# Talking-heads attention and a gated transformer on one core: mixers scaled by GpSimd, 1+exp on ScalarE, a new order of the steps

## Chip, cores and metric

The kernel runs on 1 core of a Trainium2 chip. The metric is the device time of one execution in microseconds (us); less is better.

## What is computed

Sixteen batches of 512 tokens with 256 features go through two branches. One is an attention with 16 heads of size 16, in which a 16 x 16 matrix mixes the heads before the softmax and another after it. The other is a two-layer transformer with local attention (8 heads of size 64, window of 128) and a gated feed-forward part. The second branch's output x goes through a sigmoid and gates the first.

```python
# talking heads, for each batch
logits = einsum('bhid,bhjd->bhij', rope(q), rope(k)) * SCALE
logits = einsum('bhij,gh->bgij', logits, Wpre)
attn = softmax(logits, axis=-1)
attn = einsum('bhij,gh->bgij', attn, Wpost)
out = einsum('bhij,bhjd->bhid', attn, v)      # then @ Wout.T + bout
# gate, for each of 2 layers
x = x + local_attention(l2norm(q), l2norm(k), v) @ wo
h = layernorm(shift_token(x)) @ w1 + b1
a, g = split(h); x = x + (a * gelu(g)) @ w2 + b2
# at the end: attention output times silu(x), added to the input
```

## The kernel before

Each engine runs its own instruction stream, written out by hand with semaphores. The work of a batch is cut into some 330 named steps. `ORDER` is one list of all steps of a batch (lines 124 to 156); `FIRST_ORDER` and `LAST_ORDER` are the lists of the first and the last batch. Every engine walks through the same list and issues its own part of each step, so that the list sets the order in each of the five queues. Steps in `AHEAD` belong to the next batch, steps in `BEHIND` (bound, sigmoid, silu, gated, store) to the batch before. An engine's queue is in order: an instruction that waits holds all behind it.

**Talking heads.** A tile of scores has 8 query tokens x 16 mixed heads = 128 rows and 512 keys; there are 64 tiles (`scores.0` to `scores.63`). `expand` (GpSimd, L1487) makes the queries times the mixing weights for two tiles, in two products; `part` splits them into a rounded part (ScalarE, L979) and a rest (GpSimd, L1492), three chunks ahead at most. `scores` is six matmuls (L711 to 713), a maximum on VectorE (L1220), and Exp with the row sums on ScalarE (L992). For a pair of tiles, `mixers.m` takes the reciprocal of the row sums of tiles 2m and 2m+1 on VectorE (L1206), and then multiplies the post-softmax mixing matrix by them, also on VectorE (L1211): one product of 2 x 128 elements in each row, into `mixer_n`, which has two buffers. `mix.m` is 64 small matmuls of `probs` with `mixer_n` (L728); its two banks are copied out by ScalarE and VectorE (L553). `values` (L747) and `project` (L755) follow.

**Gate.** `qkv` is 18 matmuls into banks F0 to F2; VectorE multiplies by the rotation tables (L1243), ScalarE squares, VectorE sums (L1251) and clips (L1257), GpSimd takes the power -0.5 (`inv_norms`, L1503). `join` adds the rotated halves (VectorE, L1271) and scales k (GpSimd, L1510). `q_turn` and `k_turn` (L787) transpose. `local_scores` (L805) is followed by a masked minimum on VectorE (L1303), four Exps (ScalarE, L1042), and in `weigh` a reciprocal (VectorE, L1323) and a product over 128x1024 elements (GpSimd, L1518). `p_turn` transposes (L820, copied by L1314 and L1051), `local_values` (L836, copied into `o_locT` by L1332), `out_proj` (L848). `up` with gelu and `down` (L915) end the layer.

**Output gate.** `bound` clips x (VectorE, L1420) and takes exp(-x) (ScalarE, L1099); `sigmoid.t`, four times, adds 1 (L1425) and takes the reciprocal (L1427) on VectorE. `silu` and `gated` are products on GpSimd (L1535, L1540), `store` is a DMA from GpSimd's queue (L1545).

Of the kernel before, what the change touches and what calls it, by code (L numbers as in the profile page):

```python
# [134 lines left out]
part.11 scores.20 expand.12 local_values.0.5 p_turn.0.6 part.12 mix.9 out_proj.0.2 expand.13 local_values.0.6
p_turn.0.7 scores.21 local_values.0.7 mixers.10 scores.22 part.13 out_proj.0.3 mix.10 half_turn.0 scores.23
shift_turn.0 mixers.11 project.0 scores.24 scores.25 mix.11 expand.14 part.14 h_scale.0 mixers.12 scores.26 values.2
h_turn.0 expand.15 scores.27 part.15 scores.28 expand.16 mix.12 up.0.0 up.0.1 up.0.2 up.0.3 mixers.13 part.16 up.0.4
up.0.5 scores.29 mix.13 expand.17 mixers.14 down.0.0 down.0.1 down.0.2 down.0.3 mix.14 part.17 expand.18 x_turn.1
part.18 scores.30 scores.31 expand.19 qkv.1.0 join.1.0 scores.32 mixers.15 qkv.1.1 q_turn.1.0 k_turn.1.0 part.19  # L140
scores.33 join.1.1 scores.34 mix.15 mixers.16 qkv.1.2 k_turn.1.1 join.1.2 values.3 scores.35 expand.20 q_turn.1.1
mix.16 mixers.17 part.20 qkv.1.3 q_turn.1.2 k_turn.1.2 project.1 expand.21 join.1.3 scores.36 part.21 scores.37 mix.17
scores.38 q_turn.1.3 expand.22 part.22 mixers.18 k_turn.1.3 scores.39 mix.18 local_scores.1.0 mixers.19 scores.40
scores.41 mix.19 mixers.20 local_scores.1.1 weigh.1.0 expand.23 scores.42 part.23 values.4 local_scores.1.2 p_turn.1.0
scores.43 expand.24 weigh.1.1 weigh.1.2 scores.44 mix.20 local_scores.1.3 mixers.21 local_values.1.0 p_turn.1.1
scores.45 scores.46 mix.21 local_scores.1.4 local_values.1.1 weigh.1.3 mixers.22 part.24 p_turn.1.2 weigh.1.4
scores.47 local_scores.1.5 mix.22 expand.25 out_proj.1.0 scores.48 weigh.1.5 mixers.23 local_values.1.2 part.25
p_turn.1.3 mix.23 local_scores.1.6 local_values.1.3 scores.49 p_turn.1.4 expand.26 mixers.24 part.26 scores.50
out_proj.1.1 local_values.1.4 expand.27 values.5 local_scores.1.7 mix.24 weigh.1.6 weigh.1.7 p_turn.1.5 scores.51
# [9 lines left out]
expand.0 part.0 expand.1 part.1 expand.2 qkv.0.0 part.2 join.0.0 expand.3 scores.0 scores.1 qkv.0.1 q_turn.0.0  # L159
k_turn.0.0 join.0.1 scores.2 mixers.0 qkv.0.2 mix.0 scores.3 join.0.2 q_turn.0.1 mixers.1 part.3 k_turn.0.1 expand.4  # L160
qkv.0.3 k_turn.0.2 q_turn.0.2 scores.4 join.0.3 scores.5 mix.1 part.4 scores.6 mixers.2 q_turn.0.3 k_turn.0.3 scores.7
expand.5 mix.2 part.5 mixers.3 local_scores.0.0 expand.6 scores.8 scores.9 weigh.0.0 local_scores.0.1 mix.3 scores.10
p_turn.0.0 weigh.0.1 part.6 expand.7 local_scores.0.2 values.0 local_values.0.0 mixers.4 part.7 p_turn.0.1 weigh.0.2
scores.11 mix.4 expand.8 sigmoid.0 local_scores.0.3 local_values.0.1 weigh.0.3 mixers.5 scores.12 p_turn.0.2 scores.13
part.8 expand.9 mix.5 local_scores.0.4 mixers.6 out_proj.0.0 local_values.0.2 local_scores.0.5 p_turn.0.3 scores.14
scores.15 weigh.0.4 mix.6 part.9 weigh.0.5 local_scores.0.6 local_values.0.3 mixers.7 p_turn.0.4 scores.16 mix.7
expand.10 local_scores.0.7 local_values.0.4 out_proj.0.1 weigh.0.6 weigh.0.7 scores.17 p_turn.0.5 mixers.8 scores.18
p_turn.0.6 part.10 local_values.0.5 values.1 expand.11 local_values.0.6 store out_proj.0.2 scores.19 mix.8 p_turn.0.7
part.11 expand.12 scores.20 silu mixers.9 bound part.12 local_values.0.7 scores.21 expand.13 out_proj.0.3 mixers.10
mix.9 half_turn.0 scores.22 part.13 shift_turn.0 mix.10 scores.23 scores.24 expand.14 mixers.11 part.14 expand.15  # L170
project.0 h_scale.0 scores.25 scores.26 mix.11 mixers.12 gated h_turn.0 values.2 scores.27 scores.28 mix.12 part.15
mixers.13 up.0.0 sigmoid.1 up.0.1 up.0.2 expand.16 up.0.3 part.16 scores.29 mix.13 up.0.4 up.0.5 expand.17 part.17
mixers.14 scores.30 scores.31 expand.18 down.0.0 down.0.1 down.0.2 down.0.3 mixers.15 mix.14 x_turn.1 scores.32 mix.15
part.18 qkv.1.0 join.1.0 qkv.1.1 join.1.1 q_turn.1.0 values.3 k_turn.1.0 expand.19 scores.33 qkv.1.2 k_turn.1.1
# [117 lines left out]
def gate_network_kernel(nc, a, out):  # L292
# [9 lines left out]
    with ExitStack() as ctx:  # L302
# [629 lines left out]
        def _(act):  # L932
# [717 lines left out]
```

## Time and profile before

| | us |
|---|---|
| median of 3 runs | 5370.03 |
| lowest, highest | 5368.29, 5371.4 |
| the profiled execution | 5372.07 |
| its span, first to last instruction | 5370.0 |
| busy TensorE (PE) | 5119.1 |
| busy VectorE (DVE) | 3692.1 |
| busy ScalarE (ACT) | 2659.8 |
| busy GpSimd (POOL) | 2619.2 |

The profile is of one execution. PE is TensorE with its matmuls, PEld its weight loads. The matmuls' ends are modelled, and they overlap. The granted clock is 0.994 of full speed over the span. The batches are alike, about 331 us each in the middle of the run; batch 7 (counted from 0) has its first qkv step at 2376.8 us.

### The profile page before, as it was taken

To read this page: it belongs to the slowest core of one execution; us is meant where nothing else is said; L and a number is where in the kernel's file an instruction comes from. 1 tells how busy PE (TensorE), PEld (TensorE's weight loads), DVE (VectorE), ACT (ScalarE), POOL (GpSimd) and SP (SyncE) were. 2 spreads that over 40 slices of the span, in tenths; PEclk is the share of its full clock that TensorE was granted. 3 is DMA by queue.
4 is the path that set the end of the run, shared out by engine and by line. 5 is a ranking of instruction groups with operands and counts; after the bars stand their busy time and mean duration, and the time that the engine had idled before them with its cause. 6 is when DMAs were issued, how large, how long until landed. Compare 5 with 4: busy or idle time off the path is not lost. (4 is left out here: it accounts for less than half of the span.)

```text
span 5370.0 us, 176617 instructions
## 1 busy us (share of the span) xinstructions
PE 5119.1 (95%) x72856; PEld 4155.2 (77%) x72856; DVE 3692.1 (69%) x8889; ACT 2659.8 (50%) x6551; POOL 2619.2 (49%) x2308
## 2 busy tenths in 40 slices
PE   6999999999999999999999999999999999999998
PEld 5887777877778777787777777777777777777776
DVE  6667676667766667666676666766667676676765
ACT  4445554455544454544545445454455544555544
POOL 4445554445544445444464444544445444454543
PEclk9999999999999999999999999999999999999999
DMA  2211111121111111111110111101111011111110
GB/s 79 95 66 63 46 35 64 45 67 42 38 61 56 57 41 38 61 61 53 40 64 35 61 53 51 58 31 61 54 50 58 30 61 62 42 58 39 52 49 17
DMA packets 51388, 280.78 MB, mean 52 GB/s; under 512 B 5280, under 2 KB 22688, under 8 KB 33696
## 3 DMA queue, kind: packets, MB, share of 16 engines
q1 hardware_dynamic: 39840, 252.69, 12.8%
q0 software_dynamic: 10752, 16.78, 1.7%
q8 instruction: 584, 9.57, 0.7%
q14 instruction: 212, 1.74, 0.1%
HBM read 249.01 MB, written 28.84 MB: 52 GB/s over the span
## 5 line engine op out<-in xcount | busy, mean ns | idle before, releaser
L1492 POOL TENSOR_TENSOR q_lo<-q_mix,q_hi 128x512 fp32r<-128x512 f32 x512 | 663.5, 1296 | 1349.7 <-ACT q_hi L979 1349.7
L992 ACT ACTIVATE probs<-bank_S,neg_max 128x512 f32<-128x512 f32 x1024 | 700.6, 685 | 1180.3 <-DVE neg_max L1220 993.7
L711 PE MATMUL bank_S<-k_hi,q_lo 128*128 128x512 f32 x2048 | 874.5, 427 | 9.6 <-POOL q_lo L1492 5.5
L1220 DVE TENSOR_REDUCE neg_max<-bank_S 128x1 f32<-128x512 f32 x1024 | 693.8, 684 | 263.5 <-PE bank_S L713 259.7
L713 PE MATMUL bank_S<-k_hi,q_hi 128*128 128x512 f32 x2048 | 803.9, 393 | 0.0
L712 PE MATMUL bank_S<-k_lo,q_hi 128*128 128x512 f32 x2048 | 803.5, 392 | 0.1
L728 PEld LDWEIGHTS bank_M<-mixer_n,probs 64*64 64x64 f32 x32768 | 534.1, 136 | 248.5 <-issue 161.3
L728 PE MATMUL bank_M<-mixer_n,probs 64*64 64x64 f32 x32768 | 606.1, 222 | 74.3 <-DVE mixer_n L1211 24.3
L1518 POOL TENSOR_TENSOR l_probs<-l_probs,l_inv 128x1024 f32<-128x1024 f32 (+1 forms) x256 | 428.8, 1682 | 491.7 <-DVE l_inv L1323 491.7
L1487 POOL TENSOR_TENSOR q_mix<-q_rope,w_pre 128x256 f32<-128x256 f32 x1024 | 637.6, 643 | 48.6 <-POOL q_lo L1492 1.8
L1042 ACT ACTIVATE l_probs<-l_probs,l_least 128x256 f32<-128x256 f32 (+1 forms) x1024 | 480.9, 471 | 253.0 <-DVE l_least L1303 252.6
L1503 POOL TENSOR_TENSOR inv_norms<-norms_c,minus_half 128x16 f32<-128x16 f32 x128 | 401.5, 3137 | 260.8 <-DVE norms_c L1257 260.4
L553 DVE COPY mixed<-bank_M 128x512 f32<-128x512 f32 x512 | 352.8, 689 | 230.4 <-PE bank_M L728 230.4
L711 PEld LDWEIGHTS bank_S<-k_hi,q_lo 128*128 128x128 f32 x2048 | 386.2, 189 | 114.5 <-issue 38.5
L713 PEld LDWEIGHTS bank_S<-k_hi,q_hi 128*128 128x128 f32 x2048 | 385.3, 188 | 88.5 <-issue 0.5
L712 PEld LDWEIGHTS bank_S<-k_lo,q_hi 128*128 128x128 f32 x2048 | 387.7, 189 | 60.1
L553 ACT COPY mixed<-bank_M 128x512 f32<-128x512 f32 x512 | 296.0, 578 | 221.8 <-PE bank_M L728 221.8
L1303 DVE CUSTOM_DVE_ANT_0 l_probs<-bank_F,mask,inv_norms 128x256 f32<-128x256 f32 (+1 forms) x1024 | 403.0, 447 | 0.0
L979 ACT ACTIVATE q_hi<-q_mix 128x512 fp32r<-128x512 f32 x512 | 321.5, 628 | 143.0 <-POOL q_mix L1487 125.5
L1211 DVE TENSOR_TENSOR mixer_n<-mixer,row_inv 128x128 f32<-128x128 f32 x512 | 349.6, 683 | 55.5 <-DVE row_inv L1206 3.1
L1402 DVE SCALAR_TENSOR_TENSOR att<-bank_F,b,shared 128x512 f32<-128x512 f32 x192 | 143.8, 750 | 319.6 <-ACT shared L1094 260.6
L915 PE MATMUL bank_F<-w,att 128*128 128x256 f32 x1536 | 342.2, 381 | 0.0
(143 smaller groups left out, 10133.8 us busy)
## 6 DMA issues: line engine op xcount, KB each, us to landing
w_qkv_hi<-split_qkv SPq DMA_DIRECT2D x30, 1536.0 KB, 6.9
w_qkv_lo<-split_qkv SPq DMA_DIRECT2D x30, 1536.0 KB, 6.3
w_hi<-split SPq DMA_DIRECT2D x30, 1408.0 KB, 6.2
w_lo<-split SPq DMA_DIRECT2D x30, 1408.0 KB, 7.8
w<-in_w SPq DMA_DIRECT2D x32, 768.0 KB, 4.3
w_o<-in_w_o SPq DMA_DIRECT2D x32, 512.0 KB, 5.8
x_in<-in_x POOLq DMA_DIRECT2D x16, 512.0 KB, 4.2
out_y<-in_x SPq DMA_DIRECT2D x16, 512.0 KB, 7.8
```

Of the source, the lines that this page charges most:

```text
L553: copy(to, bank[k][:].rearrange("p (t c i) -> p t c i", t=2, i=HI)).then_inc(emptied[k], 1)
L711: mm(bank[k][:], q_lo[q], k_hi[:, s, :], start=(s == 0), stop=False)
L712: mm(bank[k][:], q_hi[q], k_lo[:, s, :], start=False, stop=False)
L713: last = mm(bank[k][:], q_hi[q], k_hi[:, s, :], start=False, stop=(s == 1))
L728: last = mm(bank[f"M{r}"][keys, at:at + GH * HI], probs[rows, (2 * m + t) % PB, j * P + keys.start:j * P + keys.stop], mixer_n[rows, m % 2 ...
L992: fn(probs[:, n % PB, :], bank[k][:], ACT.Exp, bias=neg_max[:, n % 2:n % 2 + 1], accum_out=row_sum[:, n % 4:n % 4 + 1]).then_inc(emptied[k ...
L1042: fn(l_probs[:, u % LB, j, lo:], l_probs[:, u % LB, j, lo:], ACT.Exp, scale=-1.0, bias=l_least[:, u % 2, j:j + 1], accum_out=l_sum[:, u % ...
L1220: v.tensor_reduce(neg_max[:, n % 2:n % 2 + 1], bank[k][:], AX.X, ALU.max, negate=True)\
L1303: ins = v.tensor_tensor_reduce(l_probs[:, u % LB, j, lo:], bank[k][:, pair * 2 * P + lo:(pair + 1) * 2 * P], mask[:, lo:], inv_norms[:, t, ...
L1487: g.tensor_tensor(q_mix[:, s].rearrange("p m (i g) -> p (m i) g", g=GH), q[:, :, None].to_broadcast(shape), w_pre[:, None, :].to_broadcast ...
L1492: g.tensor_tensor(q_lo[:, c % QB], q_mix[:], q_hi[:, c % QB].bitcast(F32), ALU.subtract)\
L1518: g.tensor_tensor(l_probs[:, u % LB, :, lo:], l_probs[:, u % LB, :, lo:], l_inv[:, u % 2, :, None].to_broadcast([P, 4, 2 * P - lo]), ALU.m ...
```

## The change

- `mixers`: the product into `mixer_n` moves from VectorE to GpSimd, unchanged in shape (one for a pair of tiles). VectorE keeps the reciprocal. GpSimd waits for the reciprocal and for the mix of two pairs before.
- `bound`: ScalarE adds the 1 to exp(-x) in one Identity over the whole tile. `sigmoid.t` is the reciprocal alone, and the semaphore `one_plus` counts 1 a batch.
- `talk_v` on TensorE waits for the copies of x_turn, and x_turn on ScalarE waits for three fillings of bank S1 where it waited for one.
- All three orders are new. No step is added or removed.

```diff
-        one_plus = sem("one_plus", TW)
+        one_plus = sem("one_plus", 1)
...
             def talk_v(step):
+                for c in range(KC):
+                    pe.wait_ge(emptied[f"F{c}"], now.fill(("x_turn", 0), f"F{c}"))
...
-                    act.wait_ge(filled["S1"], now.fill(("talk_v",), "S1", ago=not l))
+                    for kind in ("talk_q", "talk_k", "talk_v"):
+                        act.wait_ge(filled["S1"], now.fill((kind,), "S1", ago=not l))
...
                 fn(x_mid[:], x_mid[:], ACT.Exp, scale=-1.0).then_inc(exp_done, 1)
+                act.wait_ge(exp_done, now.at(exp_done, 0))
+                fn(x_mid[:], x_mid[:], ACT.Identity, bias=1.0).then_inc(one_plus, 1)
...
                 v.reciprocal(row_inv[:, m % 2, :], row_sum[:, m % 2 * 2:m % 2 * 2 + 2]).then_inc(inv_done, 1)
-                if now.past(not (m < 2)):
-                    dve.wait_ge(filled["M1"], now.fill(("mix", (m - 2) % PAIRS), "M1", ago=m < 2))
-                dve.wait_ge(inv_done, now.at(inv_done, m + 1))
-                shape = [P, 2, GH * HI]
-                v.tensor_tensor(mixer_n[:, m % 2], mixer[:].rearrange("p g i -> p (g i)")[:, None, :].to_broadcast(shape),
-                                row_inv[:, m % 2, :, None].to_broadcast(shape), ALU.mult).then_inc(mixer_done, 1)
...
                 if not t:
-                    dve.wait_ge(exp_done, now.at(exp_done, 0))
-                v.tensor_scalar(x_mid[:, t, :], x_mid[:, t, :], 1.0, None, ALU.add).then_inc(one_plus, 1)
-                dve.wait_ge(one_plus, now.at(one_plus, t + 1 - TW))
+                    dve.wait_ge(one_plus, now.at(one_plus, 0))
                 v.reciprocal(x_mid[:, t, :], x_mid[:, t, :]).then_inc(sig_done, 1)
...
+            def mixers(step, m):
+                pool.wait_ge(inv_done, now.at(inv_done, m + 1))
+                if now.past(not (m < 2)):
+                    pool.wait_ge(filled["M1"], now.fill(("mix", (m - 2) % PAIRS), "M1", ago=m < 2))
+                shape = [P, 2, GH * HI]
+                g.tensor_tensor(mixer_n[:, m % 2], mixer[:].rearrange("p g i -> p (g i)")[:, None, :].to_broadcast(shape),
+                                row_inv[:, m % 2, :, None].to_broadcast(shape), ALU.mult).then_inc(mixer_done, 1)
```

`ORDER` at places of which the prediction speaks, old lines and new ones:

```diff
-expand.0 part.0 expand.1 part.1 bound qkv.0.0 scores.0 expand.2 join.0.0 scores.1 qkv.0.1 q_turn.0.0 join.0.1 part.2
...
-q_turn.0.1 qkv.0.3 part.4 mix.1 scores.5 q_turn.0.2 join.0.3 mixers.2 k_turn.0.2 scores.6 scores.7 expand.5 mix.2
-sigmoid.0 part.5 mixers.3 q_turn.0.3 k_turn.0.3 scores.8 scores.9 mix.3 local_scores.0.0 mixers.4 expand.6 part.6
...
-mixers.6 scores.14 scores.15 mix.6 weigh.0.3 p_turn.0.1 sigmoid.2 part.9 silu scores.16 gated sigmoid.3 mixers.7
-p_turn.0.2 local_values.0.1 local_scores.0.4 expand.10 scores.17 scores.18 out_proj.0.0 mix.7 part.10 local_scores.0.5
...
-local_values.1.6 scores.54 expand.29 mixers.26 part.29 local_values.1.7 scores.55 mix.26 mixers.27 out_proj.1.3
-expand.30 mix.27 half_turn.1 scores.56 part.30 shift_turn.1 project.2 scores.57 scores.58 values.6 mixers.28 h_scale.1
...
+mixers.1 qkv.0.3 q_turn.0.2 k_turn.0.2 join.0.3 part.4 scores.5 mix.1 bound q_turn.0.3 mixers.2 scores.6 expand.5
+k_turn.0.3 scores.7 sigmoid.0 mix.2 mixers.3 part.5 local_scores.0.0 expand.6 scores.8 scores.9 weigh.0.0 part.6 mix.3
...
+local_scores.0.3 local_values.0.1 mixers.6 weigh.0.3 scores.14 silu sigmoid.3 p_turn.0.2 gated scores.15 part.9 mix.6
+store mixers.7 local_scores.0.4 out_proj.0.0 scores.16 scores.17 local_values.0.2 p_turn.0.3 weigh.0.4
...
+p_turn.0.7 scores.22 mixers.10 part.13 local_values.0.7 scores.23 mixers.11 expand.14 mix.10 out_proj.0.3 mix.11
...
+down.0.3 mix.15 x_turn.1 scores.32 scores.33 qkv.1.0 join.1.0 part.18 mixers.16 qkv.1.1 values.3 join.1.1 k_turn.1.0
...
+part.29 mixers.26 local_values.1.7 project.2 expand.30 out_proj.1.3 scores.55 mixers.27 mix.26 half_turn.1 scores.56
+part.30 mix.27 shift_turn.1 expand.31 scores.57 scores.58 mixers.28 part.31 values.6 h_scale.1 scores.59 scores.60
```

## Rows read from the trace of the kernel before

**Rows 1.** The page: each engine's busy us, its share, its instructions.
```profile
PE 5119.1 (95%) x72856; PEld 4155.2 (77%) x72856; DVE 3692.1 (69%) x8889; ACT 2659.8 (50%) x6551; POOL 2619.2 (49%) x2308
```

**Rows 2.** Waits of PE: who waited for whom, us in total, times, longest.
```profile
PE bank_F L848 <- DVE o_locT L1332: 42.2, 14, 3.0
...
PE bank_M L728 <- DVE mixer_n L1211: 24.3, 33, 1.4
PE bank_M L728 <- DVE o_locT L1332: 19.1, 14, 1.4
PE bank_M L787 <- POOL shared L1510: 18.2, 30, 1.5
...
PE bank_M L836 <- DVE pT L1314: 13.0, 14, 0.9
PE bank_M L728 <- DVE att L1280: 11.8, 26, 0.7
```

**Rows 3.** Timeline around out_proj.0.0 of batch 7: start, us, engine, line, [idle before].
```profile
2445.56 2.35 POOL L1535 TENSOR_TENSOR x_mid<-x_mid,x_tok 128x1024 f32<-128x1024 f32 x1 [3.27 <-DVE x_mid L1427]
2445.61 2.45 DVE L1211 TENSOR_TENSOR mixer_n<-mixer,row_inv 128x128 f32<-128x128 f32 x1
...
2449.09 1.97 PE L848 MATMUL bank_F<-w_o,o_locT 128*128 128x256 f32 x8 [3.01 <-DVE o_locT L1332]
```

**Rows 4.** Timeline around mix.23 of batch 7.
```profile
2606.64 1.89 POOL L1518 TENSOR_TENSOR l_probs<-l_probs,l_inv 128x1024 f32<-128x1024 f32 x1 [1.25 <-DVE l_inv L1323]
2606.72 1.97 DVE L1211 TENSOR_TENSOR mixer_n<-mixer,row_inv 128x128 f32<-128x128 f32 x1
...
2609.16 1.16 PE L728 MATMUL bank_M<-mixer_n,probs 64*64 64x64 f32 x64 [1.36 <-DVE o_locT L1332]
```

**Rows 5.** Instructions of lines 1211 and 1487: ns min/median/max, first and last start.
```profile
L1211 DVE TENSOR_TENSOR mixer_n<-mixer,row_inv x512: 291/293/2447, 68.5 to 5344.9; 128x128 f32<-128x128 f32 x171
...
L1487 POOL TENSOR_TENSOR q_mix<-q_rope,w_pre x1024: 607/621/1682, 49.5 to 5305.2; 128x256 f32<-128x256 f32 x171
```

**Rows 6.** Groups by line: count, busy us, mean ns of one, idle before.
```profile
L1042 ACT ACTIVATE l_probs<-l_probs,l_least 128x256 f32<-128x256 f32 (+1 forms) x1024 | 480.9, 471 | 253.0 <-DVE l_least L1303 252.6
...
L1211 DVE TENSOR_TENSOR mixer_n<-mixer,row_inv 128x128 f32<-128x128 f32 x512 | 349.6, 683 | 55.5 <-DVE row_inv L1206 3.1
...
L1042 ACT ACTIVATION_READ_ACCUMULATOR l_probs<-l_probs,l_least 128x1 f32 x1024 | 192.0, 188 | 0.0
...
L1425 DVE TENSOR_SCALAR x_mid<-x_mid 128x256 f32<-128x256 f32 x64 | 41.7, 652 | 0.5 <-ACT x_mid L1099 0.5
...
L1545 POOL DMA_DIRECT2D out_y<-s_tok x16 | 21.5, 1344 | 0.3 <-POOL s_tok L1540 0.3
...
L1099 ACT ACTIVATE x_mid<-x_mid 128x1024 f32<-128x1024 f32 x16 | 17.0, 1061 | 19.1 <-DVE x_mid L1420 19.1
```

**Rows 7.** Busy us by engine of 20 us in batch 7: PE, PEld, DVE, ACT, POOL.
```profile
2437.00:2457.00 20.00, 16.73 (x342) 13.21 (x342) 18.93 (x43) 10.84 (x33) 11.21 (x8) 1.00 0.01 2
```

**Rows 8.** Timeline from mix.26 to mix.27 of batch 7.
```profile
2640.28 1.16 PE L728 MATMUL bank_M<-mixer_n,probs 64*64 64x64 f32 x64
...
2641.37 1.99 PE L848 MATMUL bank_F<-w_o,o_locT 128*128 128x256 f32 x8
...
2642.72 0.29 DVE L1211 TENSOR_TENSOR mixer_n<-mixer,row_inv 128x128 f32<-128x128 f32 x1
...
2643.29 1.15 PE L728 MATMUL bank_M<-mixer_n,probs 64*64 64x64 f32 x61
```

**Rows 9.** Timeline of PE: qkv.1.0, the step after, k_turn.1.0; then line 1503.
```profile
2534.05 0.40 PE L661 MATMUL bank_F<-w_qkv_hi,xT_hi 128*128 128x512 f32 x1
...
2538.15 0.39 PE L711 MATMUL bank_S<-k_hi,q_lo 128*128 128x512 f32 x1
...
2545.07 0.66 PE L787 MATMUL bank_M<-ident,shared 128*128 128x128 f32 x4 [0.84 <-POOL shared L1510]
...
L1503 POOL TENSOR_TENSOR inv_norms<-norms_c,minus_half x128: 2892/2901/3912, 60.1 to 5219.4; 128x16 f32<-128x16 f32 x128
```

More of the change, by code:

```diff
@@ L135 @@
[L135 to L149, printed above, removed]
@@ L156 @@
+up.1.2 mix.31 up.1.3 values.7 x_turn.0 project.3 up.1.4 up.1.5 talk_q talk_k talk_v down.1.0 down.1.1 down.1.2
+down.1.3
 """
 FIRST_ORDER = """
[L159 to L172, printed above, removed]
@@ L188 @@
-mixers.31 up.1.0 up.1.1 scale mix.31 up.1.2 up.1.3 x_turn.0 values.7 up.1.4 up.1.5 talk_q talk_k down.1.0 down.1.1
-talk_v down.1.2 down.1.3 project.3
+expand.0 part.0 expand.1 part.1 expand.2 qkv.0.0 part.2 join.0.0 expand.3 bound scores.0 scores.1 qkv.0.1 mixers.0
+q_turn.0.0 join.0.1 k_turn.0.0 part.3 expand.4 qkv.0.2 q_turn.0.1 mix.0 scores.2 scores.3 part.4 join.0.2 sigmoid.0
+k_turn.0.1 expand.5 mixers.1 qkv.0.3 k_turn.0.2 scores.4 scores.5 mix.1 q_turn.0.2 mixers.2 join.0.3 scores.6 mix.2
@@ L190 @@
+values.6 mixers.28 h_scale.1 part.31 scores.59 scores.60 mixers.29 mix.28 h_turn.1 mix.29 scores.61 scores.62
+mixers.30 up.1.0 scores.63 mixers.31 mix.30 up.1.1 up.1.2 mix.31 norm up.1.3 scale up.1.4 values.7 x_turn.0 project.3
+up.1.5 talk_q talk_k down.1.0 down.1.1 talk_v down.1.2 down.1.3
 """
 LAST_ORDER = """
-expand.0 part.0 expand.1 part.1 expand.2 bound qkv.0.0 scores.0 part.2 join.0.0 expand.3 scores.1 qkv.0.1 part.3
-expand.4 scores.2 mixers.0 k_turn.0.0 scores.3 join.0.1 mixers.1 q_turn.0.0 mix.0 part.4 qkv.0.2 q_turn.0.1 expand.5
@@ new lines @@
+expand.13 p_turn.0.7 mixers.10 part.13 scores.22 local_values.0.7 expand.14 scores.23 mixers.11 mix.10 out_proj.0.3
+part.14 half_turn.0 expand.15 mix.11 shift_turn.0 scores.24 part.15 project.0 h_scale.0 scores.25 values.2 scores.26
+mixers.12 h_turn.0 scores.27 expand.16 part.16 scores.28 mix.12 mixers.13 up.0.0 up.0.1 mix.13 up.0.2 up.0.3 up.0.4
+up.0.5 expand.17 scores.29 scores.30 mixers.14 down.0.0 down.0.1 down.0.2 down.0.3 part.17 expand.18 mix.14 x_turn.1
+part.18 scores.31 scores.32 mixers.15 qkv.1.0 mix.15 join.1.0 expand.19 qkv.1.1 scores.33 mixers.16 part.19 values.3
@@ new lines @@
+mixers.26 p_turn.1.7 scores.54 local_values.1.7 part.29 scores.55 expand.30 mix.26 mixers.27 out_proj.1.3 part.30
+project.2 half_turn.1 mix.27 shift_turn.1 scores.56 scores.57 values.6 mixers.28 h_scale.1 scores.58 scores.59 mix.28
+expand.31 mixers.29 h_turn.1 scores.60 scores.61 mixers.30 mix.29 up.1.0 part.31 mix.30 up.1.1 up.1.2 up.1.3 up.1.4
+up.1.5 scores.62 scores.63 mixers.31 down.1.0 down.1.1 down.1.2 end.silu end.gated down.1.3 end.store end.bound mix.31
+end.sigmoid.0 end.sigmoid.1 end.sigmoid.2 end.sigmoid.3 values.7 project.3
```

127 lines of the change are left out of this document (70 added, 57 removed).

## The prediction

> **What bounds the kernel now.** I read the engine totals first. PE is busy for 5119.1 of 5370.0 us and every other engine for 69% or less [rows 1]; the matmuls are the same after the change, so only PE's 251 us of idle time can be won. Next I read who ends PE's waits. Five of its waits end at an instruction of DVE and come at one or two fixed places of every batch: 42.2 us before out_proj (14 times 3.0), 24.3 and 19.1 and 11.8 before mix, 13.0 before local_values. They make 110.4 us; the waits that end at POOL's `shared` make 18.2 [rows 2].
>
> Then I followed each of the five back in the timeline of batch 7, and all lead to one instruction, DVE's `mixer_n` product (L1211). At 2445.61 it takes 2.45 us, because POOL began its silu product of 2.35 us at 2445.56; `pT` and `o_locT` stand behind it in DVE's queue, and PE waits 3.01 us for `o_locT` [rows 3]. At 2606.72 it takes 1.97 us against POOL's l_probs product of 1.89 that began 0.08 us earlier, and PE's mix waits 1.36 us for the `o_locT` copy behind it [rows 4]. Over the run L1211 has a median of 293 ns and a maximum of 2447 [rows 5], and a mean of 683 [rows 6]: it runs 512 x (683 - 293) = 200 us longer than its own work. In the stretch that holds the 3.01 us wait DVE is busy for 18.93 of 20 us, so such a delay isn't caught up [rows 7]. Reciprocals of weigh and mixers often stand next to each other on DVE, so POOL's weigh and DVE's product start together; this is a property of the order, not chance.
>
> The Trainium skill ("SBUF — State Buffer", 🔬 SBUF: two separate sides) says that DVE and GpSimd share one pair of ports, held by one of them for a whole instruction, also against a DVE instruction with two SBUF inputs. By that rule the stretch of L1211 is a block to the end of POOL's instruction; the trace agrees (1.97 us beside 1.89).
>
> **The product moves to POOL.** DVE loses 512 products, 349.6 us [rows 6], and with them the stretches. POOL gains 512 products of 256 elements with two broadcast inputs. POOL's own expand product has that size and kind of operands: median 621 ns [rows 5]. So 512 x 0.62 = 318 us, and POOL goes from 49% to about 55%. All five PE waits above are the stretch of an instruction that leaves DVE: I take them off whole, **-110 us**. Bounds: 0 if DVE is late at these places for other reasons, and -130 if the wait at k_turn (18.2) goes as well.
>
> The product itself takes 0.62 in place of 0.29 us, so it is ready 0.33 us later. Where does that reach PE? The least cover in the old order is that of mix.27, with mix.26 and out_proj.1.3 between the scores and it. Mix.26 starts at 2640.28, out_proj at 2641.37, the product ends at 2643.01 and mix.27 starts at 2643.29 [rows 8]. 0.33 later and a short hop would just miss that: 0.1 to 0.4 us late. The new order has two places with such a cover of 2.9 us (mix.11, behind mix.10 and out_proj.0.3; mix.27, behind mix.26, half_turn.1 and scores.56). 15 batches x 2 x 0.25 = **+8 us**. The rest of the 32 have 3.5 us or more.
>
> The reciprocal stays on DVE, whose wait for the product of m - 2 is long met. The new wait on POOL is for inv_done; behind it stand POOL's parts, expands, weighs and inverse norms, and PE waits for `q_lo`, `l_probs` and `k`. In the new order the product mostly comes a few steps after its second scores. The feed of `q_lo` runs up to three chunks ahead, so a wait of 1 to 2 us there is covered.
>
> **1+exp on ScalarE.** DVE loses 64 additions, 41.7 us; ScalarE gains 15 or 16 Identities over 1024 elements at the price of the Exp of the same size, 1.06 us [rows 6]. ScalarE is busy half of the time and does it beside matmuls: nothing. If that cover were gone it were 16 us. Bound itself goes from ahead of qkv.0.0 to behind mix.1. ScalarE's Exp waits there for DVE, 19.1 us in 16 times [rows 6], and now the Exps of the next scores stand behind it: nothing, up to 1.2 x 15 = 18 us if they are needed at once. After the last batch nothing covers it: at most 1.1 us, less the four additions that go. Counted in the orders, the changes between exp and gelu work on ScalarE go from 95 to 97, two loads, also beside matmuls.
>
> **The new order.** I compared the PE work that lies between a producer's step and its consumer's, in the old and the new ORDER. 18 matmuls of qkv take 2538.15 - 2534.05 = 4.1 us, 0.228 each, so a scores step is 1.4 us and the mix 1.1 [rows 8, 9].
> - k_turn.0.3 had 7.7 us behind qkv.0.3 and now has 5.1. The chain over norms, inverse norm and join held k_turn.1.0 until 2545.07, 6.9 us after its qkv step [rows 9]. POOL's inverse norm takes 2.90 us in the median and 3.91 at most, so the chain is 5.8 to 6.8 long. That is 0.7 to 1.7 late where 0.4 is lost now: +0.8. k_turn.1.0 goes from 5.9 to 6.5: -0.5. Net 0.3 x 15 = **+4 us**.
> - Of the 16 p_turns four now have 4.6 to 6.6 us behind their local_scores (before, one had under 9). The chain is four Exps with their accumulator reads, 4 x (0.471 + 0.188) = 2.6 [rows 6], the weigh product of 1.89 [rows 4], and I estimate 1.3 for DVE's first two instructions, its reciprocal and the hops: 5.8 just fits into the 6.6 of the one with whole tiles, and the other three, of window 0, have half-size tiles. One DVE instruction in front is enough to miss it. I put 0.4 us on each: 4 x 0.4 x 15 = **+24 us**; bounds 0 and 60.
> - qkv.1.1 now follows qkv.1.0 at once. Its first bank was filled 2.7 us before the step ended, its next 1.4; I cost it at nothing, 0.5 us a batch if DVE is behind.
> - Store moves ahead of mixers.7 on POOL: 1.34 us of issue [rows 6] before a mix with 9.7 us of cover. SP's loads keep their steps, each far ahead of its use; the added waits of talk_v and x_turn are for things that are over. Nothing.
>
> **Sum.** -110 + 8 + 4 + 24 = -74 us. The profiled execution took 5372.07 us for a span of 5370.0, so 5298; the median of the three timed runs is 2 us under it, so **5296 us**. DVE goes from 3692 to about 3300 us busy.
>
> **Rivals.**
> 1. *POOL's queue makes the mixes late, slower.* POOL works in order. If a weigh of 1.9 us (or its wait) stands in front of the product each time, a mix wants 3.15 + 1.9 = 5.05 us of cover (3.15 is the least cover and the 0.25 late of above). Eleven of 32 have less in the new order (2.9 twice, 3.5, 3.7, six of about 4.6, 5.0), together 9.8 us short: 15 x 9.8 = 146, so 5296 + 138 = 5434 us. With a part of 1.3 us in front it is 4.7 x 15 = 70, or 5358. It decides from about 1.4 us on. For it: POOL's load is in the same stretches as the mixes. Against: in the order only few products have a weigh between their scores and themselves. Chance 0.17.
> 2. *Shorter covers take the gain back, no change.* Almost all covers are shorter in the new order (weigh's median 12.4 to 11.6, mix's 7.4 to 6.5 us). If the same 110 us come back as many small waits of 0.2 to 0.5 us, it is 5350 to 5380. Chance 0.13.
> 3. *The block only changes its victim.* POOL has 318 us more in which it can hold DVE's remaining instructions with two SBUF inputs (join, the scalings), and DVE can hold POOL, as an inverse norm of 3.91 beside 2.90 suggests [rows 9]. If a third of the 200 us and the waits behind it stay, the gain is halved: 5335. Chance 0.09. The Trainium skill ("Perfetto Trace Analysis", Optimizing Scalar/DVE Operations) warns of this: moving work between GpSimd and DVE might not help, because they share a port. Here the moved product was the one blocked most, so I follow the rows.
> 4. *More than counted.* DVE's 391 us less also end the other waits on it, the new order places everything well, and the +24 doesn't come: 5250. Chance 0.15.
>
> **How the numbers follow.** The forecast has 0.46, with a range of its own from 5275 to 5325. The range for 8 in 10 reaches down past rival 4, where all bounds fall well, to 5235, and up into rival 1 to 5400. A measurement tells 0.2%, 11 us, from no change. Faster: 0.46 + 0.15 + 0.09 + 0.04 of rival 2 = 0.74. Same: 0.06. Slower: 0.17 + 0.03 = 0.20.
>
> **What would show it.** PE's waits for `o_locT` at 3 us are gone and its idle time is near 175 us. POOL's `mixer_n` has a median near 620 ns. DVE's busy time is about 3300. PE's waits for POOL's `mixer_n` are at few places, each under 0.5 us. k_turn.0.3 waits about 1 us. If PE's waits for POOL's `mixer_n` come to over 80 us, rival 1 is right; if `o_locT` still is 3 us late, the first term was wrong.

## The result, and the profile after

The changed kernel takes 5218.55 us (5211.75 to 5219.43, 4 runs) where the kernel before takes 5370.72: a ratio of 0.9714 with a 95% interval of 0.9698 to 0.9731. It is 152 us faster. The forecast was 5296 (74 faster) with a range from 5235 to 5400: the direction was right, half of the gain was missing, and the time lies below the range.

The page after, its span and its engines' busy us, to set beside [rows 1]:

```profile
span 5217.6 us, 176618 instructions
...
PE 5096.4 (98%) x72856; PEld 4140.1 (79%) x72856; DVE 3394.9 (65%) x8313; ACT 2670.8 (51%) x6569; POOL 2851.1 (55%) x2820
```

PE's idle time fell from 250.9 to 121.2 us, that is by 130, and its busy time by 22.7 for the same 72856 matmuls. The waits of PE after (who waited for whom: us in total, times, longest), against [rows 2]:

```profile
PE bank_M L788 <- POOL shared L1514: 35.9, 43, 1.4
PE bank_F L671 <- DVE x_in L1167: 29.6, 1, 29.6
PE bank_M L748 <- issue: 11.0, 12, 1.5
PE bank_M L729 <- issue: 10.9, 8, 2.1
...
PE bank_M L748 <- ACT mixed L552: 3.2, 1, 3.2
...
PE bank_M L729 <- POOL mixer_n L1496: 1.5, 2, 0.8
```

All five waits of [rows 2] that ended at DVE and were followed in the forecast are gone; what stands in their place at `mixer_n` is 1.5 us. `x_in` is the start of the run. The only wait that grew by more than 1 us is the one for POOL's `shared` in front of k_turn, from 18.2 to 35.9. Four lines of before that the forecast never used shrank as well:

```profile
PE bank_M L728 <- issue: 17.3, 18, 2.8
PE bank_M L747 <- issue: 16.6, 17, 1.9
PE bank_M L747 <- ACT mixed L553: 14.9, 15, 2.1
...
PE bank_M L787 <- DVE mixed L553: 6.6, 15, 1.0
```

The product on POOL (ns min/median/max), and its group (count, busy us, mean ns, idle before):

```profile
L1496 POOL TENSOR_TENSOR mixer_n<-mixer,row_inv x512: 389/402/1368, 68.5 to 5186.0; 128x128 f32<-128x128 f32 x171
...
L1496 POOL TENSOR_TENSOR mixer_n<-mixer,row_inv 128x128 f32<-128x128 f32 x512 | 216.4, 423 | 816.3 <-DVE row_inv L1210 815.0
```

It takes 0.40 us, not the 0.62 of the expand product, and the row shows why: its form is 128x128, that is 128 elements in a row, two times 64. The text ahead of the result says 2 x 128 and 256 elements; that was a misreading, and the rows of L1211 already had the right form [rows 5, 6]. The 815 us of idle POOL in front of it are time in which its queue stood still, 280 times, for DVE's reciprocal.

DVE's busy time fell to 3394.9 us and not to the forecast's 3300. Groups that stayed on DVE got longer, the clip of the norms most of all (first before, then after; its count, busy us, mean ns):

```profile
L1257 DVE TENSOR_SCALAR norms_c<-norms 128x16 f32<-128x16 f32 x128 | 27.1, 212 | 4.5
...
L1255 DVE TENSOR_SCALAR norms_c<-norms 128x16 f32<-128x16 f32 x128 | 53.0, 414 | 4.5
```

### The profile page after: what moved, and what is told of

Same layout as the page of the kernel before. It is cut to its first block, busy times and chain, and to the rows that moved or that the text cites. A ratio compares the mean times of both kernels' runs of the same rounds, so it can differ in the third digit from the quotient of the medians.

```text
span 5217.6 us, 176618 instructions
## 1 busy us (share of the span) xinstructions
PE 5096.4 (98%) x72856; PEld 4140.1 (79%) x72856; DVE 3394.9 (65%) x8313; ACT 2670.8 (51%) x6569; POOL 2851.1 (55%) x2820
## 4 chain that ended last, share of the span: by engine, by line
PE 88%; DVE 3%; issue 3%; POOL 3%; ACT 1%; POOLq 0%; DVEq 0%; ACTq 0%
PE bank_M L729 10%; PE bank_S L712 9%; PE bank_S L714 8%; PE bank_S L713 8%; PE bank_F L916 6%; PE bank_F L660 5%; PE bank_F L662 5%; PE bank_F L661 5%; PE bank_F L806 5%; PE bank_F L849 4%; PE bank_M L837 4%; PE bank_F L821 4%; PE bank_M L748 4%; PE bank_M L756 2%; DVE shared L1241 2%
## 5 line engine op out<-in xcount | busy, mean ns | idle before, releaser
L1496 POOL TENSOR_TENSOR mixer_n<-mixer,row_inv 128x128 f32<-128x128 f32 x512 | 216.4, 423 | 816.3 <-DVE row_inv L1210 815.0
L1507 POOL TENSOR_TENSOR inv_norms<-norms_c,minus_half 128x16 f32<-128x16 f32 x128 | 416.5, 3254 | 343.6 <-DVE norms_c L1255 339.8
L1241 DVE TENSOR_TENSOR shared<-bank_F,rot 128x512 f32<-128x512 f32 x512 | 324.4, 683 | 44.6 <-PE bank_F L662 44.1
```

The costliest lines, as they stand in the source:

```text
L1241: ins = v.tensor_tensor(dst[:, j, :].rearrange("p (h s d) -> p h s d", h=H, s=2), x, tab[:, None, :, :].to_broadcast([P, H, 2, HD // 2]), ...
```

## Experiments

Two theories stood against each other. A: DVE's product was blocked by POOL, and moving it away is the gain, as the forecast had it. B: the new order is the gain.

### The orders alone, and the moves alone

`e1_order_only`: the kernel before with the three new orders; the product and the four additions stay on VectorE. The added waits of `talk_v` and `x_turn` are in it too, so what it measures is the orders with them.

```diff
-ORDER, FIRST_ORDER, LAST_ORDER = (the old lists)
+ORDER, FIRST_ORDER, LAST_ORDER = (the new lists)
```

> The new orders alone: the product into mixer_n and the four additions of 1 stay on DVE as before. Theory A (DVE's product, blocked while POOL's instructions run, made the waits, and moving it away is the gain): the stretches of L1211 stay at about 200 us in total, PE still waits for DVE for 60 to 120 us, and the time is 5320 to 5390 us. Theory B (the new order is what gains): PE's waits for DVE fall under 40 us although the product is still stretched, and the time is 5240 to 5290 us.

`e2_moves_only`: the changed code with the three old lists; in the last batch `end.silu` stands behind `mix.31`.

> Both moves (product on POOL, 1+exp on ScalarE) with the old orders; in the last batch's order end.silu is put behind mix.31, since POOL would else wait for the end before its last products. Theory A: the five waits of PE that ended at DVE (110 us) fall to under 20 us, the time is 5240 to 5270 us. Theory B: the old order puts POOL's other work in front of the product, the gain is under 50 us and the time 5320 to 5370 us.

`e3_product_only`: the old lists too (with `end.silu` behind `mix.31` as in e2), and only the product moves.

> The product on POOL alone, old orders, additions of 1 still on DVE. If the product is all of the gain of the moves, it is within 5 us of the kernel with both moves. If the additions (41.7 us on DVE, up to 1.9 us for one) matter, it is 10 to 30 us slower than that one.

| | us | ratio to before | interval |
|---|---|---|---|
| new order alone (e1) | 5255.64 | 0.9781 | 0.9765 to 0.9798 |
| both moves, old order (e2) | 5438.61 | 1.0127 | 1.0107 to 1.0147 |
| product moved, old order (e3) | 5488.92 | 1.0212 | 1.0193 to 1.0230 |
| all (after) | 5218.55 | 0.9714 | 0.9698 to 0.9731 |

Theory A fails. The order alone brings 118 of the 152 us, and the moves without it cost 65. The same moves are worth 37 us with the new order and -65 with the old: a hundred us lie in how the two fit. In e1 the product is still DVE's, but hardly stretched:

```profile
L1213 DVE TENSOR_TENSOR mixer_n<-mixer,row_inv x512: 291/293/2480, 67.2 to 5217.1; 128x128 f32<-128x128 f32 x171
...
L1213 DVE TENSOR_TENSOR mixer_n<-mixer,row_inv 128x128 f32<-128x128 f32 x512 | 204.0, 398 | 55.1 <-DVE row_inv L1208 1.7 <-PE bank_M L837 0.5 <-PE bank_M L788 0.5
```

Its mean is 398 ns where it was 683 [rows 6]: 512 x (398 - 293) = 54 us beyond its own work in place of 200. The new order does not only take such overlaps apart, it also makes others: the four DVE groups that grew most from before to after, the clip of the norms, a scaling in the layernorm, and the `t_k` and first `k_rope` instructions, are 80 us longer in after, 67 us longer in e1, and no longer in e2, which has the old order. They come with the order and not with the move.

What the moves cost in the old order is seen on POOL. First the wait lines of PE in e2, then POOL in front of a mix.5 that was 2.60 us late, then POOL in e3 in front of a mix.7 (2.34 us late):

```profile
PE bank_M L728 <- POOL mixer_n L1494: 171.0, 139, 4.3
```

```profile
2454.82 1.04 POOL L1520 TENSOR_TENSOR l_probs<-l_probs,l_inv 128x512 f32<-128x512 f32 x1
2458.28 1.26 POOL L1486 TENSOR_TENSOR q_lo<-q_mix,q_hi 128x512 fp32r<-128x512 f32 x1 [2.42 <-ACT q_hi L979]
2459.50 0.40 POOL L1494 TENSOR_TENSOR mixer_n<-mixer,row_inv 128x128 f32<-128x128 f32 x1
```

```profile
2499.94 2.37 POOL L1537 TENSOR_TENSOR x_mid<-x_mid,x_tok 128x1024 f32<-128x1024 f32 x1 [3.27 <-DVE x_mid L1421]
2502.45 2.35 POOL L1542 TENSOR_TENSOR s_tok<-s_tok,x_mid 128x1024 f32<-128x1024 f32 x1
2504.75 0.41 POOL L1494 TENSOR_TENSOR mixer_n<-mixer,row_inv 128x128 f32<-128x128 f32 x1
```

The reciprocal of that mix.5 had been ready since 2456.41. The product stands behind a part, and the part waits 2.42 us for ScalarE; in e3 it stands behind silu and gated, 4.7 us of work that began with a wait for DVE. Both are not the port but the queue: the product itself takes 0.40 and 0.41 us. The difference of e3 and e2, 50 us, is what the additions on ScalarE are worth in the old order, 28 of it in PE's busy time (5157.3 against 5129.7): the forecast had costed them at nothing.

### Is it the neighbour in the queue?

`e10_two_products_first`: e2 with two pairs of neighbours exchanged. Of each pair, only GpSimd has work in both steps.

```diff
-local_scores.0.2 part.8 mixers.5 expand.9
+local_scores.0.2 mixers.5 part.8 expand.9
...
-expand.22 part.22 mixers.18 k_turn.1.3
+expand.22 mixers.18 part.22 k_turn.1.3
```

> The kernel with both moves and the old order (5438.6), with two pairs of neighbouring steps exchanged: mixers.5 ahead of part.8 and mixers.18 ahead of part.22. Only GpSimd's queue changes by that: the two products no longer stand behind a part that waits 2.4 and 1.8 us for ScalarE's rounded queries. If that waiting neighbour is what made the 2.67 and 2.65 us stalls of each batch (39 and 38 us): 5355 to 5370. If GpSimd is simply too busy in the old order: 5420 to 5440.

Measured 5344.42 (0.9950, 0.9935 to 0.9964): 94 us less than e2 for two exchanged pairs, more than the 77 of the two stalls. PE's wait for `mixer_n` fell from 171.0 to 103.6:

```profile
PE bank_M L728 <- POOL mixer_n L1494: 103.6, 112, 4.3
```

That is 67 of the 94. Another 30 are in PE's busy time, which fell from 5129.7 to 5099.6 us for the same matmuls, and its mean granted clock went from 0.991 to 0.997. Four single microseconds of e2 around the late mix.5 show where such time goes (busy us of PE, PEld, DVE, ACT and POOL, then PE's granted clock as a share of full speed):

```profile
2456.00:2457.00 1.00, 1.00 (x6) 0.78 (x5) 0.99 (x4) 1.00 (x5) 0.00 (x0) 1.00 0.00 0
2458.00:2459.00 1.00, 0.00 (x0) 0.00 (x0) 0.08 (x1) 0.87 (x3) 0.72 (x1) 1.00 0.00 0
...
2465.00:2466.00 1.00, 1.00 (x3) 0.81 (x4) 1.00 (x8) 0.86 (x3) 0.00 (x0) 0.50 0.00 0
2467.00:2468.00 1.00, 1.00 (x6) 0.84 (x5) 0.69 (x1) 0.29 (x3) 1.00 (x1) 1.00 0.00 0
```

After 2.60 us without a matmul the granted clock is 0.50, the lower of its two levels, until about 2466, and that mix takes 1.99 us where 1.16 is usual [rows 8]. Not every such wait is followed by it: after the 3.01 us of [rows 3] the clock stays at 1.00, while around the same wait one batch earlier, which ends at 2117.63, it is 0.50 from about 2116.5 to 2123.5. An estimate of the cost is the span times what the mean clock lacks of 1, good to about 3 us: 32 us in the kernel before, 21 after, 49 in e2, 77 in e3, 48 in e9, 16 in e10 and in e11. So part of what a wait costs comes behind it; no term of the forecast priced that.

`e14_six_products_first`: four more products put forward in that kernel.

```diff
-part.9 silu scores.16 gated sigmoid.3 mixers.7
+mixers.7 part.9 silu scores.16 gated sigmoid.3
-join.0.3 mixers.2
+mixers.2 join.0.3
-weigh.0.2 mixers.6
+mixers.6 weigh.0.2
-weigh.1.5 mixers.23
+mixers.23 weigh.1.5
```

> The kernel with both moves and the old order and two products put forward (5344.4), with four more put ahead of the step that stands in front of them on GpSimd: mixers.7 ahead of part.9 and silu, mixers.2 ahead of join.0.3, mixers.6 ahead of weigh.0.2, mixers.23 ahead of weigh.1.5. Their stalls are 19.2, 17.4, 17.8 and 17.0 us there. If the place in GpSimd's queue is what the moves cost in the old order: 5275 to 5295, less than with the three swaps alone and no move (5299.7). If the stalls only go to the next product: 5320 to 5345.

Measured 5292.56 (0.9856, 0.9839 to 0.9872), with 36.4 us of waits for `mixer_n` left. Three of the four stalls went; at mix.2 PE still waits about as long, now for DVE's `att` (15.6 us in all). So with the old order otherwise, the places of six `mixers` steps turn a loss of 65 us into a gain of 77. VectorE's reciprocals move with these steps, and two of the six exchanges (mixers.7 and mixers.23) are also made in the next kernel, so this is not GpSimd's queue alone. That gain is no larger than that of the next kernel, which moves nothing between engines; the intervals overlap.

`e11_three_swaps`: the kernel before, nothing moved between engines, and three pairs exchanged.

```diff
-gated sigmoid.3 mixers.7
+gated mixers.7 sigmoid.3
-weigh.0.6 weigh.0.7 mixers.9
+mixers.9 weigh.0.6 weigh.0.7
-weigh.1.5 mixers.23
+mixers.23 weigh.1.5
```

> The kernel before with three pairs of neighbouring steps exchanged: mixers.7 ahead of sigmoid.3, mixers.9 ahead of weigh.0.6 and weigh.0.7, mixers.23 ahead of weigh.1.5. VectorE then makes its product before the reciprocal that starts GpSimd's long product, so the two no longer begin together; nothing is moved between engines. Theory B (the adjacency in the order made the waits): PE's waits at out_proj.0.0 (44 us), mix.23 (20) and local_values.0.5 (15) go, 5285 to 5305. Rival (VectorE is full there, and another wait takes their place): 5330 to 5370.

Measured 5299.74 (0.9865, 0.9850 to 0.9879): 72 us for three swaps. The waits of the three places went from 42.2 to 11.9, from 19.1 to nothing and from 13.0 to nothing, and PE's busy time fell by 18 us. This shows the mechanism of [rows 3] at the places that were exchanged. The other two of the five waits were not touched and stayed (24.3, and 11.8 that became 10.2). The place of [rows 3] in this kernel:

```profile
2409.30 0.29 DVE L1211 TENSOR_TENSOR mixer_n<-mixer,row_inv 128x128 f32<-128x128 f32 x1
2409.83 1.75 DVE L1427 RECIPROCAL x_mid<-x_mid 128x256 f32<-128x256 f32 x1
2411.66 2.36 POOL L1535 TENSOR_TENSOR x_mid<-x_mid,x_tok 128x1024 f32<-128x1024 f32 x1 [3.74 <-DVE x_mid L1427]
...
2412.55 1.75 PE L848 MATMUL bank_F<-w_o,o_locT 128*128 128x256 f32 x7 [0.86 <-DVE o_locT L1332]
```

The product takes 0.29 where it took 2.45, silu starts when the product is long over, and out_proj.0.0 waits 0.86 in place of 3.01. It still waits, now for the 1.75 us reciprocal in front of the copy: the swap moves the block away, not the load. The Trainium skill ("SBUF — State Buffer", 🔬 SBUF: two separate sides) calls the shared pair of ports an exclusive lock that goes to whichever instruction starts first; these rows agree, since only the order of start was changed.

### The product off VectorE, but not onto GpSimd's queue

`e5_product_scalar`: the kernel before; `mixers` moves its product to ScalarE. One `mixers` step also stands earlier in the list, mixers.25 ahead of scores.53 (in the last batch mixers.26 ahead of scores.55).

```diff
-                v.tensor_tensor(mixer_n[:, m % 2], ...).then_inc(mixer_done, 1)
+                for t in range(2):
+                    ins = fn(mixer_n[:, m % 2, t, :], mixer[:].rearrange("p g i -> p (g i)"), ACT.Copy,
+                             scale=row_inv[:, m % 2, t:t + 1])
+                ins.then_inc(mixer_done, 1)
...
-p_turn.1.6 scores.53 expand.28 mixers.25
+p_turn.1.6 mixers.25 scores.53 expand.28
```

> The kernel before, in its old order, with the product made by ScalarE as two copies with a scale in each row; 1+exp stays on VectorE. The product can no longer be stretched by GpSimd on VectorE, and it does not stand in GpSimd's queue either. Theory A (the five waits are the stretch of this instruction and are won when it leaves VectorE): the 3.0 us in front of out_proj.0.0 are gone, 5260 to 5300. Theory B (only the order wins): 5350 to 5380; the waits then stand at other instructions. In both cases PE may wait a little for ScalarE's product, whose Exps stand in the same queue.

Measured 5317.67 (0.9896, 0.9878 to 0.9913), 54 us less than before, between the theories.

```profile
PE bank_M L726 <- ACT mixer_n L998: 49.8, 68, 1.7
...
PE bank_F L846 <- ACT pT L1058: 11.1, 14, 0.8
```

DVE's waits are gone as the forecast says, and about half of them come back at the new owner of the product, which has a queue too. The product costs two instructions of 341 ns there. What the earlier mixers.25 adds was not measured apart. So the five waits did end with the product's leaving DVE, as the first term of the sum has it, but none of the three moves tried in the old order (e2, e3, e5) kept the 110 us.

### Product or additions, load or place

`e4_new_order_product_dve`: the kernel after with the product back on VectorE. `e7_unused_dve_product`: after, and VectorE makes an unused copy of the product into a spare tile. `e8_pool_late`: after, with three unused products on GpSimd ahead of each real one. The unused products are extra work and change nothing that is computed.

```diff
 # e7, VectorE, behind the reciprocal of mixers
+                v.tensor_tensor(spare[:], (the same operands), ALU.mult).then_inc(spare_done, 1)
 # e8, GpSimd, ahead of the product of mixers
+                for i in range(3):
+                    g.tensor_tensor(spare[:], (the same operands), ALU.mult).then_inc(spare_done, 1)
```

> The kernel after with the product back on VectorE; 1+exp stays on ScalarE. It splits the 37 us that both moves together are worth in the new order (5255.6 against 5218.6). Theory P, the product on GpSimd is the gain: 5250 to 5258, as with both moves undone. Theory S, the additions on ScalarE are the gain: 5215 to 5225. With the old order the additions alone were worth 50 us (5488.9 against 5438.6), so I expect a share of both: near 5238.

> The kernel after, and VectorE also makes the same product once more behind each reciprocal, into a tile that nobody reads: VectorE has the load of the product, and its chance to be blocked by GpSimd, but nobody waits for its result. If VectorE's time in its queue is what the product costs there (others behind it late): 5235 to 5260, with waits for ScalarE's probs and the copies of VectorE. If only the place of the product itself mattered: 5216 to 5226.

> The kernel after, with three more products of the same shape on GpSimd ahead of each one that is used, into a tile that nobody reads: each used product is ready about 3 x 0.40 = 1.2 us later, and GpSimd has 614 us more work. Rival 1 of the prediction says that a mix is late by what its cover lacks. With 0.40 for the product the least cover that suffices is about 2.9 us, with the delay 4.1; the new order has 2.9, 2.9, 3.5 and 3.7 below that: 1.2 + 1.2 + 0.6 + 0.4 = 3.4 us a batch, 51 us, 5270. If GpSimd's own queue (parts, weighs, inverse norms) is late too: 5300 and more. If GpSimd has slack: under 5230.

| | us | ratio to before | interval |
|---|---|---|---|
| e4 | 5231.42 | 0.9740 | 0.9726 to 0.9755 |
| e7 | 5243.97 | 0.9763 | 0.9749 to 0.9778 |
| e8 | 5387.09 | 1.0029 | 1.0017 to 1.0041 |

e1 against e4: the additions on ScalarE are worth 24 us in the new order. e4 against after: the product on GpSimd is worth some 13, though its median is longer there (402 against 293 ns); the two were timed in different comparisons and their intervals just overlap, so this is not clear of noise. The unused products of e7 make 261 us of work on DVE (510 ns each in the mean, so partly blocked) and cost 25 us, and PE waits 19.2 us for DVE's `mixed` there, where after has no such line in front of mix. That points to time in DVE's queue as what the moves buy in the new order. Most of the additions' part sits in one wait, in e1 and then in e4:

```profile
PE bank_S L712 <- ACT probs L994: 17.5, 18, 1.1
```

```profile
PE bank_S L712 <- ACT probs L994: 2.4, 5, 1.2
```

e8 is the warning. 1.2 us more in front of each product takes back all of the gain and 16 us more. Its waits of PE:

```profile
PE bank_M L731 <- POOL mixer_n L1503: 130.0, 179, 2.2
PE bank_M L790 <- POOL shared L1521: 50.7, 58, 1.2
...
PE bank_F L823 <- POOL l_probs L1529: 12.5, 29, 0.5
```

The covers alone, as rival 1 counts them, give 51 us. PE's waits for `mixer_n` alone grew by 128.5, those for `shared` by 15 and for `l_probs` by 12.5, and PE's busy time by 21. So counting covers was too low already at the mixes, and everything else in POOL's queue is later too. POOL is busy 55% of the time in the kernel after and has almost no slack where it counts.

### The k_turn waits

`e6_k_norm_first`: after, and GpSimd's inverse norm is done in two halves, k's ahead of the scaling of k and q's behind it.

```diff
-                g.tensor_tensor(inv_norms (16 values), norms_c, minus_half, ALU.pow)
-                g.tensor_tensor(shared (k), shared, inv_norms, ALU.mult)
+                g.tensor_tensor(inv_norms (k's 8 values), norms_c, minus_half, ALU.pow)
+                g.tensor_tensor(shared (k), shared, inv_norms, ALU.mult)
+                g.tensor_tensor(inv_norms (q's 8 values), norms_c, minus_half, ALU.pow).then_inc(inv_q_done, 1)
```

> The changed kernel with POOL's inverse norm cut in two: the eight values of k first, then join's product of k, then the eight values of q. If the chain norms, inverse norm, join is what PE waits for at k_turn.0.0, 0.3 and 1.0 (35.9 us at POOL's shared, and 41 us in steps that are stretched), and the power costs by the element, the half takes 1.5 us and the waits go: 5175 to 5190 us, 30 to 45 us less than the changed kernel. If the power's time is mostly fixed per instruction, it takes 2.5 us or more twice and the time is the same or up to 20 us more.

Measured 5274.84 (0.9815, 0.9795 to 0.9834), 56 us slower than after. The wait for `shared` fell to 5.5 us, but VectorE's next clip overwrites the norms that the second half reads:

```profile
2525.58 1.64 POOL L1519 TENSOR_TENSOR inv_norms<-norms_c,minus_half 128x8 f32<-128x8 f32 x1
...
2527.35 0.17 DVE L1257 TENSOR_SCALAR norms_c<-norms 128x16 f32<-128x16 f32 x1 [2.42 <-POOL inv_norms L1519]
2527.45 0.69 DVE L553 COPY mixed<-bank_M 128x512 f32<-128x512 f32 x1
...
2528.29 0.63 PE L789 MATMUL bank_M<-ident,shared 128*128 128x128 f32 x4 [2.87 <-DVE mixed L553]
```

DVE waits 2.42 us, the copy behind it is late, and PE's next turn waits 2.87. POOL has two instructions in place of one, and PE's wait for `mixer_n` rose from 1.5 to 29.3 us as well.

`e9_k_turns_later`, `e12_two_k_turns`, `e13_q_turn_first`: after, with only `ORDER` edited.

```diff
 # e9, e12 and e13
-k_turn.0.0 q_turn.0.0 join.0.1 scores.2
+q_turn.0.0 join.0.1 scores.2 k_turn.0.0
-k_turn.0.3 scores.7
+scores.7 k_turn.0.3
 # e9 too
-k_turn.1.0 expand.19 q_turn.1.0 qkv.1.2
+expand.19 qkv.1.2 k_turn.1.0 q_turn.1.0
 # e13 too
-k_turn.1.0 expand.19 q_turn.1.0 qkv.1.2
+expand.19 q_turn.1.0 k_turn.1.0 qkv.1.2
```

> The kernel after with k_turn.0.0 behind scores.2, k_turn.0.3 behind scores.7 and the pair k_turn.1.0, q_turn.1.0 behind qkv.1.2. PE's waits for GpSimd's scaled k at these three places are 1.25 + 0.86 + 0.82 us a batch, 44 us in all. If PE can do the step in front meanwhile: 5175 to 5185. If the later copies of the turned tiles hold VectorE, ScalarE or the next join, the waits come back elsewhere: 5205 to 5240.

> The kernel after with k_turn.0.0 behind scores.2 and k_turn.0.3 behind scores.7; layer 1 stays as it is. In the kernel that moved three of them these two waits were gone, and a new one of 4.6 us stood at k_turn.1.1. Theory: a wait for GpSimd's scaled k is won by the step put in front of it where nothing stands behind the turn: 5218 - 15 x (1.25 + 0.86) = 5187, 5180 to 5195. Rival (the later copies hold the following joins and scores in layer 0 as well): 5205 to 5220.

> The same, and q_turn.1.0 ahead of k_turn.1.0, both still ahead of qkv.1.2: q_turn's 0.46 us of matmuls fill a part of the 0.82 us that k_turn.1.0 waits. If q is ready by then: 0.4 to 0.5 x 15 = 7 us less than without it, about 5180. If VectorE's copy of k then holds the next join, as where both stood behind qkv.1.2 (4.6 us at k_turn.1.1): 5190 and more.

e9 takes 5284.37 (0.9837, 0.9821 to 0.9854), 66 us more than after. All three waits went, and a worse one came at k_turn.1.1:

```profile
PE bank_M L786 <- DVE att L1276: 62.5, 14, 4.7
```

```profile
2518.45 1.23 DVE L1267 TENSOR_TENSOR shared<-shared 128x1024 f32<-128x1024 f32 x1 [3.27 <-PE bank_F L786]
```

DVE's join of the next tile writes the buffer that the late turns still read, so it waits 3.27 us for PE. Behind it in DVE's queue stand 2.5 us of rotation products and 1.5 of norm sums, and only then, at 2523.74, the copy `att` that PE's next turn waits for. 21 of the 66 us are in PE's busy time. e12, with the two turns of layer 0 alone, takes 5201.22 us (0.9687, 0.9672 to 0.9701), some 17 us less than after and the best kernel of this study; the two were not timed in one comparison, and their intervals touch. Its waits:

```profile
PE bank_M L728 <- DVE att L1277: 14.5, 14, 1.0
...
PE bank_M L787 <- POOL shared L1513: 11.7, 15, 1.0
```

24 us of the waits for `shared` went, and 14.5 came back at DVE's copy of k. e13 takes 5203.00 (0.9691, 0.9676 to 0.9705): no difference to e12 that can be told. Its wait for `shared` did fall, from 11.7 to 3.1 us, but PE's busy time in the profiled execution is 13 us more (5101.5 against 5088.0).

## Why the prediction was right or wrong

The step that failed is the price of the new order. The forecast put it at +28 us (4 for k_turn, 24 for the p_turns) and the two moves at -102 (-110 and +8, and nothing for the additions). Measured, the order alone is -118 (e1), and the moves on top of it are -37, of which the additions are 24. The two errors in part cancel; what is left put the time below the range.

- *PE's idle time is the bound.* Mostly right: 130 us of the gain are idle time. That nothing else can be won was wrong: PE's busy time fell by 23 for the same matmuls.
- *The five DVE waits lead to the stretch of L1211.* Right. e11 shows it for three of them by three swaps. For the other two the trace of before has the product at 1.97 and 1.12 us in batch 7, and e5 shows only that they end when it leaves DVE.
- *The move takes them off, -110.* The size is right, since 110.4 became about nothing, but the cause is not, and here the price of the order went wrong. The forecast says that the adjacency is a property of the order and then does not look at how the new order places those pairs. It takes the pairs apart by itself (e1: -118, with the product still on DVE).
- *The product prolonged to 0.62, +8.* 0.40 measured, and PE waits 1.5 us for it. The forecast took the product for one of 256 elements like expand's, where the form beside its own name, 128x128, says 128 [rows 5]. The price was half too high by a row misread, not by a property of the chip.
- *Four p_turns with short cover, +24.* Nothing came; in the kernel after, PE idles 0.2 us in front of the matmuls of p_turn:

```profile
L821 PE MATMUL bank_F<-ident,l_probs 128*128 128x128 f32 x1792 | 249.3, 279 | 0.2 <-issue 0.2
```

The chain of 5.8 us was worked out for whole tiles and the extra 0.4 for each was a guess about DVE's queue. The bound of 0 was right.
- *k_turn, +4.* +18. The two turns that the forecast followed wait 0.62 and 0.75 us in batch 7, near the forecast. The one that it did not follow, k_turn.0.0, had no wait before and has one of 1.08 now: 14 or 15 times a us, the whole difference.

```profile
2331.32 0.66 PE L788 MATMUL bank_M<-ident,shared 128*128 128x128 f32 x4 [1.08 <-POOL shared L1514]
...
2352.94 0.66 PE L788 MATMUL bank_M<-ident,shared 128*128 128x128 f32 x4 [0.62 <-POOL shared L1514]
...
2486.99 0.66 PE L788 MATMUL bank_M<-ident,shared 128*128 128x128 f32 x4 [0.75 <-POOL shared L1514]
```

- *The additions on ScalarE, nothing.* Wrong: 24 us in the new order, 50 in the old. The forecast asked what they cost on ScalarE and not what DVE's queue gains.
- *DVE falls to 3300 us.* It fell to 3395, because other groups on DVE were stretched in the new order (80 us in four groups, 67 of them already in e1).
- *What the sum left out.* The two issue lines (33.9 to 21.9), ACT's `mixed` (14.9 to 3.2), DVE's `mixed` (6.6 to 0.4), ACT's `probs` (4.2 to 0.3) and PE's busy time (22.7) make 57 us. With the 32 of the two terms that did not come, less 14 more at k_turn, that is 75 of the 78 that were missing. How the 57 divide among the three parts of the change is open in part. The order alone (e1) has the issue lines (18.2), ACT's `mixed` (2.1) and PE's busy time (5098.8), but not ACT's `probs` (17.5), which went with the additions (2.4 in e4). About 11 of the 22.7 us of busy time are the granted clock, by the estimate above (32 and 21). Part of the busy time is at matmuls that follow a wait: out_proj's took 401 ns in the mean and take 389.
- *Rival 1 (POOL's queue, slower).* It did not come, but it is no bad mechanism: it is what e2 and e3 do (+65, +115), and what e8 does with 1.2 us more. The forecast put the decision point at 1.4 us; e8 shows that it lies below 1.2. What saved the change is the order.
- *Rival 2 (small waits take the gain back).* Not in after: its idle time is 121 us in all. In the old order it is what e5 does, where 61 us came back in 82 small waits.
- *Rival 3 (the block changes its victim).* Not as stated: POOL's product is 423 ns in the mean against a median of 402, 11 us in all, and its move in the old order (e2) left DVE's other groups as they were. The new order did give DVE other victims (the 80 us above). Whether they cost PE anything, at k_turn for one, whose chain the clip of the norms is part of, was not tested. The Trainium skill ("Perfetto Trace Analysis", Optimizing Scalar/DVE Operations) says that moving work between GpSimd and DVE might not help because of the shared port. With the old order it did not help, but the rows put that down to the queue, not the port: e10 and e14 have the same product on GpSimd as e2, and take 94 and 146 us less.
- *Rival 4 (more than counted, 5250)* was what happened, at a larger size. It had a chance of 0.15, and the range ended 16 us above the time.

## What to carry to other kernels

When engines walk one list in order, a move between engines and a new list are not separate terms: price the move at the place of each instruction in its new queue, and ask which of the old waits the new list takes away alone. A stretched instruction can be cured by exchanging it with its neighbour, here 72 us for three swaps, before anything is moved. A wait is won by the step put in front of it only if nobody waits for the buffer that the late step reads. And a long wait of TensorE can cost again behind itself, when its granted clock falls.

## What the runs showed of the hardware

- Two-input products on GpSimd took 402 ns for 128 elements in a row (`mixer_n`, after) and 621 for 256 (`q_mix` [rows 5]), medians of 512 and 1024 instructions. An estimate from the two is 1.7 ns for an element and 0.18 us for the rest.
- GpSimd's power -0.5 took 2.90 us over 16 values in a row (median [rows 9]) and 1.64 over 8 (single instructions in e6); an estimate from the two is 0.16 us for a value and 0.4 for the rest.
- TensorE's granted clock fell to 0.50 of full speed after some waits of 2.6 to 4.4 us (they end at 2459.95 in e2 and at 2524.58 in e9) and stayed there for 3 to 7 us; after the 3.01 us of [rows 3] it did not fall.
- The block works both ways: the same power took 3.91 us in e9 at 2508.87, where the median before is 2.90, while DVE's join with two SBUF inputs ran from 2508.79 to 2510.02:

```profile
2508.79 1.23 DVE L1267 TENSOR_TENSOR shared<-shared 128x1024 f32<-128x1024 f32 x1
...
2508.87 3.91 POOL L1505 TENSOR_TENSOR inv_norms<-norms_c,minus_half 128x16 f32<-128x16 f32 x1 [17.39 <-DVE norms_c L1253]
```
